# A graph layer with mixture of experts on one core: number table of the compares in PSUM, row scaling shared by two engines, first indices without the codes

## What is computed

```python
deg_out = clip(segment_sum(ones, src), 1); deg_in = clip(segment_sum(ones, dst), 1)
h = feats * rsqrt(deg_out)[:, None]
m = segment_sum(h[src], dst) * rsqrt(deg_in)[:, None]
x = m @ W_gc + b_gc + feats @ W_res + b_res
y = x + moe_top2(x)          # 64 experts, 256 -> 512 (gelu) -> 256, gates of the two best
out = layernorm(feats + batchnorm(y) * gamma + beta)
```

## Time and profile before

| | us |
|---|---|
| median of the runs | 3272.07 |
| the profiled execution | 3275.65 |
| its span, first to last instruction | 3273.9 |
| start, up to the first gather | 234 |
| gather stage, first to last gather | 2146 |
| experts, from the first token gather | about 665 |
| norms | about 194 |

### The profile page before, as it was taken

The page is one execution under the profiler, slowest core; times in us unless marked ns, Lnnn a source line. Parts: engine busy times, 40 slices in busy tenths (PEclk is TensorE's granted clock), DMA queues, the critical chain, the costliest instruction groups (busy, mean ns, idle before and its releaser), DMA issues.

```text
span 3273.9 us, 45262 instructions
## 1 busy us (share of the span) xinstructions
PE 2161.2 (66%) x10294; PEld 1770.7 (54%) x10295; DVE 1260.3 (38%) x3117; ACT 387.2 (12%) x1329; POOL 2160.5 (66%) x2118
## 2 busy tenths in 40 slices
PE   7935556556566666666666767777767887879460
PEld 7934444444444454455554555555546776878350
DVE  9961111122223233343444444545541122222377
ACT  0000000000000000010111111111111222223113
POOL 1017777777777777777777777777735566666603
PEclk6556777777878787888888888889978899989775
DMA  7023333333333333333333333333333455555332
GB/s 267 0 90 99 97 96 100 96 99 98 98 98 101 98 99 97 99 98 103 100 100 100 101 102 101 102 98 103 101 97 124 131 164 154 169 156 170 123 113 78
DMA packets 205281, 362.36 MB, mean 111 GB/s; under 512 B 43337, under 2 KB 126071, under 8 KB 205055
## 3 DMA queue, kind: packets, MB, share of 16 engines
q0 software_dynamic: 93888, 230.63, 24.4%
q1 hardware_dynamic: 104110, 123.31, 11.8%
q10 hardware_dynamic: 7056, 6.43, 0.6%
HBM read 328.57 MB, written 57.52 MB: 118 GB/s over the span
## 4 chain that ended last, share of the span: by engine, by line
POOL 52%; issue 22%; PE 12%; DVE 6%; DMA 4%; POOLq 2%; DVEq 1%; ACT 1%; PEld 1%; ACTq 0%; PEldq 0%; SPq 0%
POOL ring L463 24%; POOL stage L463 22%; POOL ring L490 4%; PE bank L1134 3%; PE bank L1263 2%; PE bank L1269 2%; PE bank L1154 2%; POOL y L506 2%; DMA ring<-nodes,slot_idx 2%; DVE acc L1047 1%; DMA stage<-y 1%; DVE stage L761 1%; POOLq L539 1%; PE bank L1194 1%; PE bank L1256 1%
## 5 line engine op out<-in xcount | busy, mean ns | idle before, releaser
L463 POOL DMA_INDIRECT ring<-table,ring_idx x792 | 841.8, 1063 | 274.9 <-issue 240.2
L463 POOL DMA_INDIRECT stage<-table,ring_idx x776 | 826.1, 1065 | 236.4 <-issue 234.7
L1154 PE MATMUL bank<-stage 128*128 128x257 f32 x1040 | 317.7, 472 | 195.5 <-DMA stage<-table,ring_idx 188.3
L1154 PE MATMUL bank<-ring,hot 128*128 128x257 f32 x1056 | 313.9, 462 | 177.4 <-DMA ring<-table,ring_idx 170.0
L1154 PEld LDWEIGHTS bank<-stage 128*128 128x128 f32 x1040 | 246.3, 243 | 261.8 <-issue 164.7
L1154 PEld LDWEIGHTS bank<-ring,hot 128*128 128x128 f32 x1056 | 243.5, 237 | 242.0 <-issue 148.3
L952 DVE TENSOR_TENSOR acc<-acc,bank 128x257 f32 x196 | 83.0, 423 | 657.5 <-PE bank L1154 635.8
L506 POOL DMA_INDIRECT y<-ring,slot_idx x192 | 192.4, 1002 | 115.3 <-issue 91.4
L1154 PE MATMUL bank<-ring,stage 128*128 128x257 f32 x528 | 175.2, 503 | 132.0 <-DMA ring<-table,ring_idx 104.7
L490 POOL DMA_INDIRECT ring<-nodes,slot_idx x192 | 198.4, 1033 | 96.2 <-POOL slot_idx L486 56.0
L1263 PEld LDWEIGHTS bank<-ring,stage 128*128 128x128 f32 x1984 | 241.3, 199 | 12.4 <-issue 6.3
(11 more groups left out here) (228 smaller groups left out, 2618.2 us busy)
## 6 DMA issues: line engine op xcount, KB each, us to landing
stage<-in_L_gnn_w_dram SPq DMA_DIRECT2D x128, 512.0 KB
ring<-table,ring_idx POOLq DMA_INDIRECT x792
y<-zeros SPq DMA_DIRECT2D x49, 256.0 KB, 2.1
stage<-y SPq DMA_DIRECT2D x14, 896.0 KB, 7.1
stage<-table,ring_idx POOLq DMA_INDIRECT x776
stage<-in_L_gnn_b_dram SPq DMA_DIRECT2D x64, 128.0 KB
table<-stage SPq DMA_DIRECT2D x7, 896.0 KB, 4.2
nodes<-yS ACTq DMA_DIRECT2D x49, 128.0 KB
```

Source lines behind the costliest of these rows:

```text
L463: pool.indirect_dma_start(out=ring(q)[:, j, 0:D], out_offset=None, in_=table[:, :], in_offset=bass.IndirectOffsetOnAxis(ap=ring_idx[:, q, ...
L1154: last = pe.matmul(bank[:, 0:D + 1], hots[:, j, :], ring(q)[:, j, :], start=j == 0, stop=j == CPG - 1)
```

## The change

The table of numbers that the one-hot compares read is copied once into the unused last quarter of PSUM bank 5 (`iota_ps`), and L842 and L856 read it there instead of `iota_b` in SBUF. `loT` and `hiT` move from `acc` into `hot_low` and `slots`; so POOL clears all but two pieces of `acc` at once (behind `iota_n`, which now comes first) and the other two as soon as the edge lists are read. The histogram runs 49 batches and no empty 50th. `scaled` has six buffers, three in `stage` and three in the ring; DVE scales groups 0, 2, 4, 6 and ACT groups 1, 3, 5; only group 6 waits for a store (the first). The two small DMAs of `rng` go from SP's queue to ACT's, behind ACT's scaling. The ones column of the ring is written behind the stores. ACT waits for `code_ready` behind its first six index sets, no longer ahead of them.

```diff
-        loT = acc_flat[:, 2 * COLS:2 * COLS + COLS // 2].bitcast(BF16)
-        hiT = acc_flat[:, 2 * COLS + COLS // 2:3 * COLS].bitcast(BF16)
+        loT = hot_low[:, :, :].rearrange("p j d -> p (j d)")[:, 0:COLS // 2].bitcast(BF16)
+        hiT = slots[:, 0:2, :].rearrange("p a s -> p (a s)").bitcast(F32)[:, 0:COLS // 2].bitcast(BF16)
...
-        scaled = stage[:, 0:2 * TG * D].rearrange("p (b t d) -> p b t d", b=2, t=TG)
+        scaled = [home[:, b * GB:(b + 1) * GB].rearrange("p (t d) -> p t d", t=TG)
+                  for home in (stage, ring_flat) for b in range(3)]
+        SCALED = len(scaled)
...
+        iota_ps = banks[5][:, 3 * P:4 * P]
...
-            sp.wait_ge(mm_red, 1)
-            sp.dma_start(rng[0:1, 0, :], rng_f[:, 0, :]).then_inc(mm_row, 16)
-            sp.dma_start(rng[0:1, 1, :], rng_f[:, 1, :]).then_inc(mm_row, 16)
-
             for g in range(NB):
-                sp.wait_ge(h_ready, g + 1)
+                sp.wait_ge((h_ready, ha_ready)[g % 2], g // 2 + 1)
...
-                sp.dma_start(tv, scaled[:, g % 2, :, :]).then_inc(table_buf[g % 2], 16)
+                sp.dma_start(tv, scaled[g % SCALED]).then_inc(table_rest if g else table_first, 16)
...
-            pool.memset(acc_flat[:, 3 * COLS:], 0.0).then_inc(acc_zero, 1)
-            pool.iota(iota_n, pattern=[[1, P], [0, HB]], base=0, channel_multiplier=0,
+            pool.iota(iota_n, pattern=[[1, LO], [0, HB]], base=0, channel_multiplier=0,
                       allow_small_or_imprecise_dtypes=True).then_inc(const_p, 1)
-            pool.wait_ge(rs_ready, 1)
-            pool.memset(ring_low[:, :, :, D:D + 1], 1.0).then_inc(const_p, 1)
-            pool.memset(acc_flat[:, 0:3 * COLS], 0.0).then_inc(acc_zero, 1)
-            pool.wait_ge(const_p, 8)
+            pool.memset(acc_flat[:, 2 * COLS:], 0.0).then_inc(acc_zero, 1)
+            pool.wait_ge(srch_f, 2)
+            pool.wait_ge(dst_f, 1)
+            pool.memset(acc_flat[:, 0:2 * COLS], 0.0).then_inc(acc_zero, 1)
...
-            for q in range(2):
-                pool.wait_ge(table_buf[q], 16 * ((NB + 1 - q) // 2))
+            pool.wait_ge(table_first, 16)
+            pool.wait_ge(table_rest, 16 * (NB - 1))
+            pool.memset(ring_low[:, :, :, D:D + 1], 1.0).then_inc(const_p, 1)
+            pool.wait_ge(const_p, 8)
...
+            act.wait_ge(x_loaded, 32)
+            act.wait_ge(rs_ready, 1)
+            for g in range(1, NB, 2):
+                for t in range(TG):
+                    tile = g * TG + t
+                    last = act.activation(scaled[g][:, t, :], xs[:, tile, :], ACT.Identity, scale=rs[:, tile:tile + 1])
+                last.then_inc(ha_ready, 1)
+            act.wait_ge(mm_red, 1)
+            act.dma_start(rng[0:1, 0, :], rng_f[:, 0, :]).then_inc(mm_row, 16)
+            act.dma_start(rng[0:1, 1, :], rng_f[:, 1, :]).then_inc(mm_row, 16)
             act.wait_ge(b1_t, 1)
...
-            act.wait_ge(code_ready, 1)
...
             for q in range(LEAD):
                 indices(0, q, True)
+            act.wait_ge(code_ready, 1)
...
-            with dve.Fori(1, HSTEPS) as i:
+            with dve.Fori(1, HBATCH // HQ) as i:
                 hist(i, False)
+            hist(HBATCH // HQ, False, HBATCH % HQ)
...
             scale_nodes(0)
-            scale_nodes(1)
+            scale_nodes(2)
...
-            for g in range(2, NB):
-                scale_nodes(g)
+            scale_nodes(4)
+            scale_nodes(6)
...
+            dve.tensor_copy(iota_ps, iota_f[:, :])
+            dve.drain()
...
-                dve.tensor_tensor(hot[q % HOTS], iota_b[:, :].unsqueeze(1).to_broadcast([P, CPG, P]),
+                dve.tensor_tensor(hot[q % HOTS], iota_ps.unsqueeze(1).to_broadcast([P, CPG, P]),
                                   dstq[:, q % HOTS, :].unsqueeze(2).to_broadcast([P, CPG, P]), ALU.is_equal).then_inc(hot_ready, 1)
...
-                        dve.tensor_tensor(hotx[:, :, :], iota_b[:, :].unsqueeze(1).to_broadcast([P, CPG, P]),
+                        dve.tensor_tensor(hotx[:, :, :], iota_ps.unsqueeze(1).to_broadcast([P, CPG, P]),
                                           dstx[:, :].unsqueeze(2).to_broadcast([P, CPG, P]), ALU.is_equal).then_inc(hotx_ready, 1)
```

More of the change, by code:

```diff
@@ L34 @@
 HQ = 2
-HSTEPS = -(-(-(-EDGES // P)) // (HQ * HB))
 SLOTCH = CAP // P
@@ L46 @@
 DK, HK = D // P, H // P
+LO = P
+HI = NPAD // LO
+HBATCH = -(-(-(-EDGES // P)) // HB)
 def graph_moe_kernel(nc, x, src, dst, W_gc, b_gc, W_res, b_res, Wg, bg, w1, b1, w2, b2, gamma, beta, out):
@@ L189, in graph_moe_kernel @@
         banks = [ctx.enter_context(nc.psum_tensor(f"bank{i}", [P, 512], F32)) for i in range(8)]
-        lo_hot = stage[:, 0:HQ * HB * P // 2].bitcast(BF16).rearrange("p (b n c) -> p b n c", b=HQ, c=HB)
-        hi0 = HQ * HB * P // 2
-        hi_hot = stage[:, hi0:hi0 + HQ * HB * NT // 2].bitcast(BF16).rearrange("p (b t c) -> p b t c", b=HQ, c=HB)
+        lo_hot = stage[:, 0:HQ * HB * LO // 2].bitcast(BF16).rearrange("p (b n c) -> p b n c", b=HQ, c=HB)
+        hi0 = HQ * HB * LO // 2
+        hi_hot = stage[:, hi0:hi0 + HQ * HB * HI // 2].bitcast(BF16).rearrange("p (b t c) -> p b t c", b=HQ, c=HB)
         ring_flat = ring_low[:, :, :, :].rearrange("p a b c -> p (a b c)")
-        iota_n = ring_flat[:, 0:P * HB // 2].bitcast(BF16).rearrange("p (n c) -> p n c", c=HB)
-        s0 = 2 * TG * D
+        iota_n = ring_flat[:, 0:LO * HB // 2].bitcast(BF16).rearrange("p (n c) -> p n c", c=HB)
+        GB = TG * D
+        s0 = 3 * GB
         SFX = 656
@@ L213, in graph_moe_kernel @@
         h_ready = sem("h_ready")
-        table_buf = [sem("table_buf0"), sem("table_buf1")]
+        ha_ready, table_first, table_rest = sem("ha_ready"), sem("table_first"), sem("table_rest")
         acc_zero = sem("acc_zero")
@@ L733, in _ @@
             flat = raw_src[:, :, :].rearrange("p b e -> p (b e)")
-            dve.tensor_scalar(s_lo, flat, P - 1, None, ALU.bitwise_and)
+            dve.tensor_scalar(s_lo, flat, LO - 1, None, ALU.bitwise_and)
             dve.drain()
@@ L752, in _, with hist @@
             dve.wait_ge(const_p, 7)
-            def hist(i, first):
-                for q in range(HQ):
+            def hist(i, first, n=HQ):
+                for q in range(n):
                     if not first:
@@ L778, in scale_nodes @@
             def scale_nodes(g):
-                if g >= 2:
-                    dve.wait_ge(table_buf[g % 2], 16 * (g // 2))
+                if g >= SCALED:
+                    dve.wait_ge(table_first, 16)
                 for t in range(TG):
                     tile = g * TG + t
-                    last = dve.tensor_scalar(scaled[:, g % 2, t, :], xs[:, tile, :], rs[:, tile:tile + 1], None, ALU.mult)
+                    last = dve.tensor_scalar(scaled[g % SCALED][:, t, :], xs[:, tile, :], rs[:, tile:tile + 1], None, ALU.mult)
                 last.then_inc(h_ready, 1)
@@ L1126, in _, with hist @@
             last.then_inc(mm_tr, 1)
-            def hist(i, first, final=False):
-                for q in range(HQ):
+            def hist(i, first, n=HQ, final=False):
+                for q in range(n):
                     pe.wait_ge(hots_ready, i * HQ + (q + 1))
                     for c in range(HB):
-                        last = pe.matmul(banks[0][:, 0:NT], lo_hot[:, q, :, c], hi_hot[:, q, :, c],
-                                         start=first and q == 0 and c == 0, stop=final and q == HQ - 1 and c == HB - 1,
+                        last = pe.matmul(banks[0][:, 0:HI], lo_hot[:, q, :, c], hi_hot[:, q, :, c],
+                                         start=first and q == 0 and c == 0, stop=final and q == n - 1 and c == HB - 1,
                                          skip_group_check=True)
@@ L1138, in _ @@
             hist(0, True)
-            with pe.Fori(1, HSTEPS - 1) as i:
+            with pe.Fori(1, HBATCH // HQ) as i:
                 hist(i, False)
-            hist(HSTEPS - 1, False, True)
+            hist(HBATCH // HQ, False, HBATCH % HQ, True)
             pe.wait_ge(mm_row, 32)
```

12 lines of the change are left out of this document (6 added, 6 removed).

## The result

The changed kernel takes 3172.33 us, the median of 4 runs (3171.03 to 3173.34), against 3270.39 us (3266.98 to 3274.97, 4 runs) for the kernel before beside it: a ratio of 0.970, 95% interval 0.968 to 0.972. That is 98 us less, where 102 were forecast. Its profiled execution took 3172.06 us, with a span of 3170.3.

The account below looks back on a forecast made before the run. POOL's 1568 gathers, duration plus pause, bound the kernel's gather stage. Gathers 85.8 plus start 17 less 1 at the tight end make 101.8 us, from the profiled 3275.65 to 3173.9, so 3170 for the median; range 3155 to 3203.

Parts of the forecast that it names:

- Gathers: Gather stage: with the compares' table in PSUM every gather takes its median 1.009 us, 85.8 us less in all.
- Compare: DVE's compares: time unchanged at 1.23 us with a PSUM operand, argued from 1.06 ns a column and 0.15 us fixed cost.
- Start: Before the first gather: it starts near 217 in place of 233.95, a gain of 17 us, between 9 and 20.
- The first clearing grows by 1664 columns ... 1.4 us: Start, POOL's clearing: longer by 1.4 us, so DVE's work on src and the whole histogram start 1.4 us later.
- They stand behind the 21 scalings and go at 204.7: Start, ACT's queue: the two small DMAs are issued only after ACT's 21 tile scalings, at 204.7.
- a landing in 2.8 us: Start: the small DMAs land 2.8 us after issue, as on idle queues, so at 207.5, with code ready at 213.5.
- the one between POOL's ones and the first gather: End of the start: POOL gets the table at 216.0, writes the ones (0.14 us) and starts at about 216.7.
- The tight end: Last 280 us of the gather stage: PE's slack nearly used up, 1 us lost, up to 10 for the range.
- That length or result type holds the gathers: Rival on the gathers: the compare's fp32 result or length slows them; only the start gains, 3255 us; chance 0.07.
- Taken over in part: Rival on the gather stage: PE and DVE partly become the bound, 3180 to 3240 us; chance 0.08.
- The slower case: Rival: PE and DVE bound the stretch from 1400 us; a 3 us compare gives about 3295 us; chance 0.03.
- That the start doesn't do what it says: Rival on the start: small DMAs wait for slower stores, no gain; 3268 us with gathers unchanged too; chance 0.02.

Follow-up runs that it names:

- the late clearing: The changed kernel with POOL's whole clearing of acc moved behind the reading of the edge lists: 3162.03 us, 0.966 of the kernel before.
- The table alone: The kernel before with only the compares' table in PSUM: 3181.61 us, ratio 0.972; in two other sets 1.005 and 1.004.
- the two operand experiments: The changed kernel with the compares' table back in SBUF, once as fp32 (3661.32 us), once as bf16 with the small operand in PSUM (3720.75 us).
- the three late sets: Three of the five sets of experiment runs, in which the kernel before took 3664 to 3734 us in place of 3272 to 3275.
- run 61: Not a label: "In this run 61 additions" counts 61 late additions in the kernel before with only the table in PSUM, 3738.85 us against 3720.81.

## Why the prediction was right, and where it was not

**Gathers.** Forecast 85.8 us less; 89.6 measured. The price was set with the median of one half of the gathers (1.009); after the change all of them average 1.0066. The median moves that much from trace to trace (1.006 in the second trace of the kernel before). The gain is within the 92.1 that the shortest gather gave.

**Compare.** Forecast unchanged, 1.225 us measured. The value was right, but the argument for it shows nothing: a line drawn through two instructions always leaves both the same fixed cost, whatever a PSUM operand costs. That it costs nothing here is shown by the three forms that ran: 1.225 us with the table in PSUM, 1.221 with the small operand there, 1.225 with both in SBUF.

**Start.** Forecast 17 us, 16.4 measured at the first gather, with two steps wrong and one too short. `rs` was ready at 194.05 (193.9), the first store went at 196.10 (196.0) and the last landed at 216.4 (216.0); 14 scalings took 3.77 us in place of 7.83, so these steps held.

The first failed step is "The first clearing grows by 1664 columns ... 1.4 us". The work on `src` starts 2.05 us later. The row shows the reason: DVE's `ident`, a tensor_scalar, starts at 2.52 and ends at 14.26, right behind POOL's clearing (14.18), and three small constants follow it before `src`. POOL itself ends 1.3 us later (14.18 against 12.87), as forecast; the other 0.7 us are the small constants, which now stand behind it. In the trace before, the same hold is there in two parts, which the earlier trace rows do not show:

```profile
2.52 6.21 DVE L722 TENSOR_SCALAR ident<-iota_f,pcol 128x128 f32<-128x128 f32 x1
...
9.12 3.80 DVE L727 TENSOR_SCALAR inval<-valid 128x49 f32<-128x49 f32 x1
```

`ident` ends at 8.73, behind POOL's clearing (8.65), and `inval` at 12.92, behind its table (12.87). DVE wasn't waiting for a result of POOL's last instruction, as I read the earlier trace rows; its own instructions were held while POOL ran. So the question was not how long the clearing grows but whether it has to be there, and the late clearing shows 7.7 us in that.

The second is "They stand behind the 21 scalings and go at 204.7". ACT's queue issued the small DMAs at 199.06 and 200.50 while ACT was still scaling, until about 202.7. The next step, a landing in 2.8 us, failed the other way: from the first issue to PE's multiply of the row it took 7.0 us (199.06 to 206.03), counted as the 2.8 were, beside the stores. The codes came at 212.0 in place of 213.5. With the DMAs issued 1.8 us later, in the kernel whose scaling is all on DVE, the row landed at the same moment (PE's multiply of it starts at 206.13, against 206.18 and 206.26 in the others of its set): its issue did not set the landing. That the stores ahead of it did is likely, but no run shows it. None of it cost anything, because the table landed last. The step that was too short is the one between POOL's ones and the first gather: 0.96 us, where some 0.6 were allowed.

**The tight end.** Forecast 1 us lost, up to 10 allowed; 5.9 measured (13.1 - 7.2). The sign that the prediction gave for "taken over", the last addition more than 10 us behind the last gather, did show. It was set too low: 7.2 us stood there before the change. In the timeline after, PE at the last tick and the last group:

```profile
2270.32 0.20 PE L1183 MATMUL bank<-picked,tri 128*128 128x64 bf16 x1 [1.86 <-DVE deg L887]
...
2273.86 2.07 PE L1213 MATMUL bank<-wgc,tS 128*128 128x256 f32 x4 [0.96 <-ACT tS L623]
...
2278.14 3.70 PE L1173 MATMUL bank<-ring,hot 128*128 128x257 f32 x16
...
2282.20 3.72 PE L1173 MATMUL bank<-stage 128*128 128x257 f32 x16 [0.37 <-issue]
```

and in that of the late clearing:

```profile
2258.91 0.20 PE L1183 MATMUL bank<-picked,tri 128*128 128x64 bf16 x1 [1.86 <-DVE deg L887]
...
2261.71 1.13 PE L1213 MATMUL bank<-wgc,tS 128*128 128x256 f32 x4 [0.96 <-ACT tS L623]
...
2263.93 3.70 PE L1173 MATMUL bank<-ring,hot 128*128 128x257 f32 x16
...
2267.99 3.72 PE L1173 MATMUL bank<-stage 128*128 128x257 f32 x16 [0.37 <-issue]
```

In neither does the last group wait for its rows: at the very end PE is now the bound, as the slack in the earlier trace rows said. The tick takes 2278.14 - 2270.32 = 7.82 us after, and 5.02 in the other, where the same four matmuls take 1.13 us and not 2.07. The granted clock tells why:

```profile
2264.00:2270.00 6.00, 3.83 (x17) 2.95 (x16) 1.61 (x4) 0.00 (x0) 4.47 (x6) 1.00 0.21 60
2270.00:2278.00 8.00, 6.72 (x24) 5.07 (x24) 4.08 (x22) 1.99 (x6) 2.74 (x3) 0.58 0.06 17
2278.00:2286.00 8.00, 7.55 (x34) 5.99 (x33) 3.62 (x13) 0.99 (x4) 0.00 (x0) 1.00 0.01 3
```

The columns are the stretch, its length, busy time of PE, PEld, DVE, ACT and POOL, the granted clock, DMA share and GB/s. The clock was 0.58 during the tick, mostly its lower level of 1.2 GHz, and 1.00 on both sides. So of the 5.9 us between these two traces 2.8 are the clock in that tick; the other 3.1 are PE's distance behind POOL when the tick began (it begins 3.0 us ahead of the last gather's end, and 6.2 with the late clearing). The trace before has the same 7.2 us by another way: its last group waited 3.7 us for its rows, and its 16 matmuls took 5.42 us in place of 3.72, at a granted clock of 0.68. The table alone ended 8.0 us behind its last gather and the late clearing 7.2, so the loss belongs to a trace more than to the kernel.

**The sum.** 89.8 us in the gather stage and 16.4 at the start make 106.2. Of these 6.0 go back between the last gather and POOL's first work on the experts, and 3.4 come from experts and norms, which no edit touches: 103.6 us of span. The experts' own length moves by as much between traces (683.2 us from POOL's readiness to the start of the norms, 685.2 before, 680.5 with the table alone, 685.2 with the late clearing), so these 3.4 are no gain of the change. The medians differ by 98 us and not 103.6, because the trace of before lies 5 us above its own median here. That the sum of 101.8 us comes so near is in part luck: against the forecast the gather stage gave 4.0 us more and experts and norms 3.4, while the end gave 5.0 less and the start 0.6.

**The rivals.** That length or result type holds the gathers fell with the trace after and with the two operand experiments. "Taken over in part" was right about the place and small in size. The slower case needed a compare of 2.7 us; its own formula gives some 3310 us for one of 3 us, not 3295 (1.77 x 1.25 x 89 - 140.9 = 56 us more, on 3255). That the start doesn't do what it says is refuted by a first gather at 217.6 to 217.7 in five kernels with different tables.

## What to carry to other kernels

A median beside a maximum of twice its size is worth pairing, meeting by meeting, with what another engine does at that moment: that found 87 us that no wait shows, since the held instruction only looks long. Where one engine holds another, move one operand, or move the one instruction that nobody needs yet (a clearing) to a stretch whose instructions it doesn't hold. And a step timed from the end of another engine's instruction needs the reason for that end: a wait and a hold look alike at the next instruction, and react differently to a reordering.

## What the runs showed of the hardware that was not expected

In the three late sets the gather stage of every profiled kernel is longer by some 340 to 530 us, with the usual start (210 to 234 us), about the same experts, and gathers as short as ever; two sets with the same chip number even differ. PE's mean granted clock is lower there, 0.76 to 0.77 against 0.80 to 0.82, but a group's 16 matmuls still take 6.4 us where the waits below are of 24 us and more. The waits of the table-alone kernel in the first set (total us, times, longest) and its timeline:

```profile
DVE acc L957 <- remote: 574.6, 45, 33.9
```

```profile
257.07 6.37 PE L1159 MATMUL bank<-ring,stage 128*128 128x257 f32 x16 [4.13 <-DMA ring<-table,ring_idx]
...
287.86 0.42 DVE L957 TENSOR_TENSOR acc<-acc,bank 128x257 f32 x1 [30.53 <-remote]
...
324.28 0.42 DVE L957 TENSOR_TENSOR acc<-acc,bank 128x257 f32 x1 [33.92 <-remote]
325.49 1.00 POOL L465 DMA_INDIRECT ring<-table,ring_idx  x1 [7.58 <-DVE acc L957]
```

PE ends a group at 263.44, but its semaphore update is recorded at 287.73, and DVE adds only then; POOL meanwhile fills the ring, and stops at 317.9 for want of a free buffer. In this run 61 additions start over 2 us behind PE's last matmul with DVE idle, some 590 us in all; in both kernels' usual traces none does. Updates of DVE and ACT come promptly where they are recorded, but a part of them is missing from these traces (160 are there for 190 compares). The two kernels of that set whose compares hold POOL and that were profiled are less hit (29 and 27 late additions, 355 and 313 us) and are the faster ones there, with 16 us of that from their start. One could think that PE's signals are held up while gathers follow each other without a gap. But in the usual sets they do that too and nothing is late, and the update at 287.73 came with the gathers still running. No experiment took it apart: the cause stays open, as does what differs between the sets. What is shown is that in such a set shorter gathers gain nothing (1.005 and 1.004 for the table alone): there POOL waits for additions that start late.
